# Moving four bn_stats instructions on VectorE behind the transposed exponentials, in a cross-attention and mixture-of-adapters kernel

## Chip, cores and metric

The kernel runs on one core of one Trainium2 chip. The metric is the device time of one execution in microseconds, the median of several executions.

## What is computed

There are 8 batches of 224 query rows and 750 context rows, all of width 2048, in fp32. The first part is a cross-attention whose keys are also its values; the second is a linear layer with a low-rank expert term.

```python
# x: (8, 224, 2048)   ctx: (8, 750, 2048)
n = layernorm(x)                              # mean and variance over the 2048 columns
a = einsum('bqd,bkd->bqk', n, ctx)
c = einsum('bqk,bkd->bqd', softmax(a), ctx)
x = x + c
m = layernorm(x)
base = einsum('bsi,oi->bso', m, base_w) + base_b
hidden = einsum('bsi,ri->bsr', m, A)          # r = 64
probs = softmax(einsum('bsi,ei->bse', m, router_w))   # e = 16, the two best are kept
delta = einsum('bse,bsr,eor->bso', combine(top2(probs)), hidden, B)
out = x + base + 0.5 * delta
```

## The kernel before

Every fp32 product is made of three fp32r products: each operand is split into a high part, which ScalarE (ACT) makes by copying, and a low part, which VectorE (DVE) makes by subtracting the high part from the original. TensorE (PE) then multiplies high by high, high by low and low by high.

The attention runs over the batches, one call of `one(b, stage)` in each engine's own program. Batch 0 is the stage "first", batches 1 to 6 are the stage "mid" (a loop), batch 7 is "last". The queue of transfers is on SyncE (SP). An engine works through its list strictly in the written order and meets the others only through semaphores.

A mid batch goes like this on PE. `scores_of` multiplies the normalised queries with the context (L715 to L717). Then come the transposes of the second layer norm's rows of the batch before (L752), nine of the 16 steps of the product with A and the router (`hidden_of`, L768 to L770), the transposes of the exponentials (`exps_T`, L795), and the other seven steps of `hidden_of`. In `outputs_of` PE waits until both low parts of the transposed exponentials are there (`eT_l`, L1162), and then goes through 24 value blocks e = 0 to 23, six blocks of 128 context rows for each of four chunks of 512 columns. A block takes six matmuls (L818 to L820, three for each half of the rows). Behind block 1 come two small transposes, and ahead of blocks 13, 14, 16 and 17 the transposes of the next batch's queries. In the stage "first" there is no old batch, and so no `hidden_of` and no second layer norm between the scores and the value blocks.

Block e needs the low part of its values, `raw_l`, which DVE makes in `value_low(e)` (L1176) from `val_h`, made by ACT in `value_high(e)` (L979). `val_h` has four buffers, so ACT can begin with block e when PE has finished block e - 4. Blocks 0 to 3 are prepared while the scores run.

The next batch's first layer norm is made in between. `stats` (L1180) is one bn_stats over 512 columns of `xn`; there are eight (two halves of the rows, four chunks). Then DVE aggregates them and adds epsilon at e = 6 (`ve`, L1188), GpSimd (POOL) takes the reciprocal root (`rs`, L1570), DVE makes the shift `nb` at e = 8 (L1193), and ACT waits for it in its list between `value_high(9)` and `value_high(10)`, where it normalises the first half of `xn` (L970, 2 us); the second half follows behind `value_high(10)`.

`residual(b, c)` (L1206 and L1212) is on DVE behind `value_low(6 * (c + 1) + 3)`: it takes the finished chunk out of PSUM and adds it to `x2`, which holds the batch's input rows. Its transfer is started on SP at L523.

Of the kernel before, what the change touches and what calls it, by code (L numbers as in the profile page):

```python
# [36 lines left out]
def as_f32(ap):  # L37

    return ap.bitcast(F32)
# [24 lines left out]
def xattn_ffn_kernel(nc, x, ctx, bias, ctxT, arT, wT, bT, out):  # L64
# [129 lines left out]
    with ExitStack() as stack:  # L194
        def sb(name, shape, dt=F32, of=stack):
            return of.enter_context(nc.sbuf_tensor(name, shape, dt))
# [13 lines left out]
        def sem(name):  # L210
            return stack.enter_context(nc.semaphore(name))
# [5 lines left out]
        st1 = sb("st1", [QT, NQ, CH, STATS])  # L217
# [26 lines left out]
        with ExitStack() as first:  # L244
            xn = sb("xn", [QT, NQ, D], F32, first)
# [108 lines left out]
        xn_loaded = sem("xn_loaded")  # L354
# [17 lines left out]
        stat1, aggr1, var1, rstd1, bias1 = (sem(f"ln1_{n}") for n in ("stats", "aggr", "var", "rstd", "bias"))  # L372
# [784 lines left out]
        def _(dve):  # L1157
            def low(stage, b, name, n, high_part, low_part, cols, width):

                dve.wait_ge(high_done, act_no(stage, b, name, n) + 1)  # L1160
                src = place(stage, name, n).rearrange("p (k c) -> p k c", k=cols)[:, :, 0:width]
                dve.tensor_tensor(low_part, src, as_f32(high_part), ALU.subtract).then_inc(drained, 1)  # L1162

            def ctx_low(b, j):
                dve.wait_ge(ctx_high_done, b * NPC + j + 1)
                dve.tensor_tensor(ctxT_l[:, j % LR, :, :], ctxT_in[:, j % LR, :, :],  # L1166
                                  as_f32(ctxT_h[j % HR][:, :, :]), ALU.subtract).then_inc(ctx_ready, 1)

            def four_blocks(tile, n):
                return tile[:, 4 * n:4 * n + 4, :].rearrange("p (k i) c -> p k (i c)", k=2)  # L1170

            def value_low(b, e):
                c, t = e // NT, e % NT
                dve.wait_ge(val_high, b * (CH * NT) + e + 1)
                rows = rows_of(t)
                dve.tensor_tensor(raw[0:rows, c, t, :], raw_in[0:rows, c, t, :], as_f32(val_h[0:rows, e % NR, :]), ALU.subtract).then_inc(val_ready, 1)  # L1176

            def stats(tile, st, sem_stat, i):
                q, c = i // CH, i % CH
                dve.bn_stats(st[:, q, c, :], tile[:, q, c * BANK:(c + 1) * BANK]).then_inc(sem_stat, 1)  # L1180

            def aggregate(st, mv, sem_aggr):
                for q in range(NQ):
                    dve.bn_aggr(mv[:, q, :], st[:, q, :, :].rearrange("p c s -> p (c s)")).then_inc(sem_aggr, 1)

            def variance(mv, ve, sem_aggr, sem_var, n):
                dve.wait_ge(sem_aggr, n * NQ + NQ)
                dve.tensor_scalar(ve[:, :], mv[:, :, 1], EPS, None, ALU.add).then_inc(sem_var, 1)  # L1188

            def shift(mv, rs, nb, sem_rstd, sem_bias, n):  # L1190

                dve.wait_ge(sem_rstd, n + 1)
                dve.scalar_tensor_tensor(nb[:, :], mv[:, :, 0], -1.0, rs[:, :], ALU.mult,  # L1193
                                         ALU.mult).then_inc(sem_bias, 1)

            def row_max(b):
                for q in range(NQ):
                    dve.wait_ge(scores_done, b * NQ + q + 1)
                    dve.reduce_max(nmax[:, q:q + 1], all_scores(q), AX.X,
                                   negate=True).then_inc(max_ready, 1)  # L1200
# [15 lines left out]
            def hidden_out(stage, b):  # L1216
                dve.wait_ge(filled, job_no(stage, b, "hid") + 1)
                dve.tensor_copy(hT[:, :], hid_place(stage)).then_inc(drained, 1)
# [112 lines left out]
            def one(b, stage):  # L1331
                old, new = stage != "first", stage != "last"
                x2T_low = lambda n: low(stage, b, "x2T", n, four_blocks(nT_h, n), four_blocks(nT_l, n), 2, 2 * LQ)
                for j in range(NPC):
                    if j >= HR:
                        ctx_low(b, j)
                    if stage == "first" and j in (2, 3):
                        low("pre", 0, "qT", j, four_blocks(nT_h, j), four_blocks(nT_l, j), 2, 2 * LQ)

                    if old and j < 2:  # L1340
                        if j == 0:
                            dve.wait_ge(x2_done, b * (NQ * CH))
                        for i in range(4 * j, 4 * j + 4):
                            stats(x2, st2, stat2, i)
                        if j == 1:
                            dve.wait_ge(stat2, b * (NQ * CH))
                    if old and j == 2:
                        aggregate(st2, mv2, aggr2)
                        variance(mv2, ve2, aggr2, var2, b - 1)
                    if old and j == 3:  # L1350
                        shift(mv2, rs2, nb2, rstd2, bias2, b - 1)
                    if stage == "first" and j == 3:
                        dve.wait_ge(ar_high, 1)
                        dve.tensor_tensor(ar_l[:, :, :], ar_in[:, :, :], as_f32(ar_h[:, :, :]),
                                          ALU.subtract).then_inc(ar_ready, 1)

                    if old and j >= NPC - 2:
                        x2T_low(j - (NPC - 2))
                    if j >= NPC - 2:
                        value_low(b, 2 * (j - (NPC - 2)))  # L1360
                        value_low(b, 2 * (j - (NPC - 2)) + 1)
                if old:
                    x2T_low(2)
                row_max(b)
                if old:
                    x2T_low(NX - 1)
                if new:
                    dve.wait_ge(xn_loaded, b * 16 + 16)
                    for i in range(4):
                        stats(xn, st1, stat1, i)  # L1370
                for q in range(NQ):
                    three = lambda tile: tile[:, q, :, :].rearrange("p (k i) c -> p k (i c)", k=2)
                    low(stage, b, "eT", q, three(eT_h), three(eT_l), 2, 3 * QT)
                if old:
                    hidden_out(stage, b)
                for e in range(NR, CH * NT):
                    value_low(b, e)
                    c, t = e // NT, e % NT
                    if new and e in (4, 5):
                        for i in range(2 * e - 4, 2 * e - 2):  # L1380
                            stats(xn, st1, stat1, i)
                        if e == 5:
                            dve.wait_ge(stat1, b * (NQ * CH) + 2 * NQ * CH)
                    if new and e == 6:
                        aggregate(st1, mv1, aggr1)
                        variance(mv1, ve1, aggr1, var1, b + 1)
                    if new and e == 8:
                        shift(mv1, rs1, nb1, rstd1, bias1, b + 1)
                    if old and e == HN_AT + 3:
                        hidden_back(stage, b)  # L1390
                    if not new and e in FIRST_W_AT:
                        weight_low(FIRST_W_AT.index(e))
                    if not new and e in FIRST_A_AT:
                        tile_low(0, (FIRST_A_AT.index(e),))
                    if new and e - 3 in QT_AT:
                        n = QT_AT.index(e - 3)
                        low(stage, b, "qT", n, four_blocks(nT_h, n), four_blocks(nT_l, n), 2, 2 * LQ)
                    if c >= 1 and t == 3:
                        residual(b, c - 1)
                    if not new and c >= 1 and t in (4, 5):  # L1400
                        if t == 4:
                            dve.wait_ge(x2_done, b * (NQ * CH) + c * NQ)
                        stats(x2, st2, stat2, (t - 4) * CH + c - 1)
                if new:
                    for j in range(HR):
                        ctx_low(b + 1, j)
                residual(b, CH - 1)

            def weight_low(n):
                dve.wait_ge(w_high, n + 1)  # L1410
                loaded, high_part, low_part = w_pair(n)
                dve.tensor_tensor(low_part, loaded, as_f32(high_part), ALU.subtract).then_inc(w_ready, 1)  # L1412
# [98 lines left out]
            for g in range(GT):  # L1511
                c, i = chunk_of(g), step_of(g)
# [221 lines left out]
```

## Time and profile before

| | |
|---|---|
| median of three runs | 1424.84 us (1423.66 to 1428.0) |
| time of the profiled execution | 1423.66 us |
| its span, first to last instruction | 1421.8 us |
| PE busy | 1354.5 us, 95% of the span |
| DVE busy | 935.6 us, 66% |
| ACT busy | 623.4 us, 44% |
| mean granted clock of PE | 0.993 |
| attention, first batch to the last value block | from 0 to about 670 us |
| one mid batch | about 81 us |

A row of a timeline has the start in microseconds, the duration, the engine, the line, the operation with its output and inputs, the count of merged instructions and, in brackets, how long the engine had been idle before and what it waited for. Successive instructions overlap in the records: the next may start a little before the one in front of it ends. The time of the execution is 1.86 us longer than its span. The granted clock is 1.00 when PE runs at 2.4 GHz and 0.50 at 1.2 GHz.

### The profile page before, as it was taken

The page shows a single profiled execution, that of the slowest core. Times are in us where ns is not written, and L with a number is a line of the kernel's source. Part 1 is how long each engine was busy: PE and PEld are TensorE (multiplying, and loading weights), DVE is VectorE, ACT ScalarE, POOL GpSimd, SP SyncE. Part 2 cuts the span into 40 slices and gives each one's busy share as a digit, 9 for nine tenths or more (in the row PEclk, how much of TensorE's full clock was granted, in tenths as well). Part 3 has the DMA queues.
Part 4 walks back from the last instruction along what each step waited for, and adds up shares of the span by engine and source line. Part 5 has one row for each costly group of instructions (what it writes and reads, how often), then busy time and mean ns, then how long its engine had stood idle before and what let it go on. Part 6 is the DMA issues. An engine that isn't in the chain of part 4 may idle for free.

```text
span 1421.8 us, 18364 instructions
## 1 busy us (share of the span) xinstructions
PE 1354.5 (95%) x6777; PEld 1104.8 (78%) x6777; DVE 935.6 (66%) x1179; ACT 623.4 (44%) x777; POOL 316.9 (22%) x247
## 2 busy tenths in 40 slices
PE   5899999999999999999999999988889999999998
PEld 4678888787878888786888877777677888888886
DVE  5576768788777768768465566766667745644543
ACT  3355554545564554546321366766666400100110
POOL 2002002020201102020615724434443011111110
PEclk9899999999999999999999999999999999999999
DMA  8957678687867768679658697999995988788783
GB/s 289 296 198 255 213 251 254 211 253 255 272 222 247 250 219 250 229 247 212 208 149 205 195 300 225 301 312 298 280 286 126 329 257 255 239 255 254 229 264 125
DMA packets 206520, 345.34 MB, mean 243 GB/s; under 512 B 26912, under 2 KB 119072, under 8 KB 196768
## 3 DMA queue, kind: packets, MB, share of 16 engines
q1 hardware_dynamic: 187872, 277.06, 64.3%
q0 software_dynamic: 10528, 52.85, 12.1%
q10 hardware_dynamic: 8064, 14.68, 3.0%
q8 instruction: 35, 0.57, 0.2%
q14 instruction: 21, 0.17, 0.0%
HBM read 260.87 MB, written 99.41 MB: 253 GB/s over the span
## 4 chain that ended last, share of the span: by engine, by line
PE 37%; DMA 12%; DVE 3%; issue 1%; ACT 1%; POOL 0%; SPq 0%; POOLq 0%; ACTq 0%; DVEq 0%
PE scores L849 11%; PE scores L851 11%; PE scores L850 11%; DMA res<-x_scratch 6%; DMA y_scratch<-y_out,yrow_i 4%; PE work L885 1%; PE work L886 1%; DMA w_in<-in_wT_dram 1%; DMA a_in<-xT_scratch 1%; DVE raw_l L1176 1%; ACT y_out L1077 1%; DVE w_l L1412 0%; DVE a_l L1421 0%; DVE x L1212 0%; ACT b_hl L1069 0%
## 5 line engine op out<-in xcount | busy, mean ns | idle before, releaser
L849 PE MATMUL scores<-w_h,a_h 128*128 128x512 f32 x896 | 351.9, 393 | 3.0 <-issue 3.0
L851 PE MATMUL scores<-w_h,a_l 128*128 128x512 f32 x896 | 350.9, 392 | 0.0
L850 PE MATMUL scores<-w_l,a_h 128*128 128x512 f32 x896 | 350.5, 391 | 0.0
L1053 ACT ACTIVATE a_h<-a_in 128x512 fp32r<-128x512 f32 x148 | 83.6, 622 | 319.4 <-DMA a_in<-xT_scratch 226.0
L849 PEld LDWEIGHTS scores<-w_h,a_h 128*128 128x128 f32 x896 | 168.5, 188 | 40.3 <-issue 3.4
L851 PEld LDWEIGHTS scores<-w_h,a_l 128*128 128x128 f32 x896 | 168.4, 188 | 37.5
L850 PEld LDWEIGHTS scores<-w_l,a_h 128*128 128x128 f32 x896 | 168.5, 188 | 37.0
L1421 DVE TENSOR_TENSOR a_l<-a_in,a_h 128x512 fp32r<-128x512 f32 x148 | 113.6, 814 | 122.6 <-ACT a_h L1053 119.2
L1176 DVE TENSOR_TENSOR raw_l<-raw_in,val_h 128x512 fp32r<-128x512 f32 x192 | 155.7, 828 | 49.6 <-ACT val_h L979 48.7
L715 PE MATMUL scores<-ctxT_h,nT_h 128*112 128x494 f32 (+1 forms) x512 | 174.9, 342 | 6.9 <-DVE x L1212 3.3
L717 PE MATMUL scores<-ctxT_h,nT_l 128*112 128x494 f32 (+1 forms) x512 | 171.7, 335 | 0.0
L716 PE MATMUL scores<-ctxT_l,nT_h 128*112 128x494 f32 (+1 forms) x512 | 171.5, 335 | 0.0
L979 ACT ACTIVATE val_h<-raw_in 128x512 fp32r<-128x512 f32 x192 | 119.0, 626 | 107.6 <-PE scores L820 107.6
L1166 DVE TENSOR_TENSOR ctxT_l<-ctxT_in,ctxT_h 128x1500 fp32r<-128x1500 f32 x64 | 109.5, 1719 | 85.9 <-ACT ctxT_h L957 85.2
L1593 POOL TENSOR_TENSOR res<-res,bias_b 128x512 f32<-128x512 f32 x56 | 82.0, 1465 | 372.5 <-DMA res<-x_scratch 361.5
L818 PE MATMUL scores<-val_h,eT_h 128*112 128x512 f32 (+1 forms) x384 | 156.2, 407 | 8.1 <-DVE eT_l L1162 5.8
L820 PE MATMUL scores<-val_h,eT_l 128*112 128x512 f32 (+1 forms) x384 | 152.4, 397 | 0.0
L819 PE MATMUL scores<-raw_l,eT_h 128*112 128x512 f32 (+1 forms) x384 | 152.1, 396 | 0.0
L957 ACT ACTIVATE ctxT_h<-ctxT_in 128x1500 fp32r<-128x1500 f32 x64 | 92.2, 1451 | 118.6 <-PE scores L717 108.3
L1464 DVE TENSOR_TENSOR b_hl<-b_in,b_hl 64x2048 fp32r<-64x2048 f32 x43 | 101.0, 2351 | 63.3 <-ACT b_hl L1069 62.5
L1586 POOL TENSOR_TENSOR xT_st<-nT_h,nT_l 128x896 f32<-128x896 f32 x32 | 72.5, 2272 | 167.8 <-DVE nT_l L1162 167.8
L1570 POOL TENSOR_TENSOR rs<-ve,mhalf 112x2 f32<-112x2 f32 x16 | 15.0, 936 | 425.1 <-DVE ve L1188 425.1
(149 smaller groups left out, 1971.5 us busy)
## 6 DMA issues: line engine op xcount, KB each, us to landing
ctxT_in<-in_ctxT_dram SPq DMA_DIRECT2D x64, 750.0 KB, 7.2
raw_in<-in_ctx_dram SPq DMA_DIRECT2D x32, 1280.0 KB
a_in<-xT_scratch SPq DMA_DIRECT2D x37, 1024.0 KB, 9.0
w_in<-in_wT_dram SPq DMA_DIRECT2D x32, 512.0 KB, 9.6
x<-in_x_dram SPq DMA_DIRECT2D x8, 1792.0 KB, 9.6
xT_scratch<-xT_st SPq DMA_DIRECT2D x8, 1792.0 KB, 11.9
res<-x_scratch SPq DMA_DIRECT2D x56, 256.0 KB, 7.5
y_add<-y_scratch SPq DMA_DIRECT2D x56, 256.0 KB, 5.5
```

The costliest lines, as they stand in the source:

```text
L715: pe.matmul(out, qh, ch, start=(k == 0), stop=False)
L716: pe.matmul(out, qh, cl, start=False, stop=False)
L717: last = pe.matmul(out, ql, ch, start=False, stop=(k == KD - 1))
L818: pe.matmul(out, eh, vh, start=(t == 0), stop=False)
L819: pe.matmul(out, eh, vl, start=False, stop=False)
L820: last = pe.matmul(out, el, vh, start=False, stop=(t == NT - 1))
L849: pe.matmul(o, ah, wh, start=(k == 0), stop=False)
L850: pe.matmul(o, ah, wl, start=False, stop=False)
L851: last = pe.matmul(o, al, wh, start=False, stop=(k == KD - 1))
L979: act.activation(val_h[0:rows, e % NR, :], raw_in[0:rows, c, t, :], ACT.Copy).then_inc(val_high, 1)
L1176: dve.tensor_tensor(raw[0:rows, c, t, :], raw_in[0:rows, c, t, :], as_f32(val_h[0:rows, e % NR, :]), ALU.subtract).then_inc(val_ready, 1)
L1421: dve.tensor_tensor(a_l[at][:, cols, :], a_in[at][:, cols, :], as_f32(a_h[at][:, cols, :]), ALU.subtract).then_inc(a_ready, 1)
```

## The change

Four of the eight `stats` of the next batch's `xn`, with the wait for the transfer of `xn` ahead of them, are moved on DVE from their place ahead of the low parts of the transposed exponentials to the place behind `value_low(4)` and `value_low(5)`. Four stood there altogether before, two behind each; after the change eight do, four behind each. This holds for the stages "first" and "mid". Nothing else is changed.

```diff
@@ -1364,10 +1364,6 @@
                 row_max(b)
                 if old:
                     x2T_low(NX - 1)
-                if new:
-                    dve.wait_ge(xn_loaded, b * 16 + 16)
-                    for i in range(4):
-                        stats(xn, st1, stat1, i)
                 for q in range(NQ):
                     three = lambda tile: tile[:, q, :, :].rearrange("p (k i) c -> p k (i c)", k=2)
                     low(stage, b, "eT", q, three(eT_h), three(eT_l), 2, 3 * QT)
@@ -1377,7 +1373,9 @@
                     value_low(b, e)
                     c, t = e // NT, e % NT
                     if new and e in (4, 5):
-                        for i in range(2 * e - 4, 2 * e - 2):
+                        if e == 4:
+                            dve.wait_ge(xn_loaded, b * 16 + 16)
+                        for i in range(4 * (e - 4), 4 * (e - 4) + 4):
                             stats(xn, st1, stat1, i)
                         if e == 5:
                             dve.wait_ge(stat1, b * (NQ * CH) + 2 * NQ * CH)
```

## Rows read from the trace of the kernel before

**Rows 1.** Who waited for whom, PE, 150 to 640 us: total, times, longest.

```profile
PE scores L768 <- ACT prob L984: 3.4, 6, 0.6
PE scores L715 <- DVE x L1212: 2.8, 6, 0.5
PE scores L715 <- DVE ctxT_l L1166: 2.2, 6, 0.4
```

**Rows 2.** Timeline, PE, batch 2: the first matmul of value blocks 0, 6 and 11.

```profile
228.34 0.45 PE L818 MATMUL scores<-val_h,eT_h 128*112 128x512 f32 x1
...
236.88 0.40 PE L818 MATMUL scores<-val_h,eT_h 128*112 128x512 f32 x1
...
243.87 0.40 PE L818 MATMUL scores<-val_h,eT_h 110*112 110x512 f32 x1
```

**Rows 3.** Timeline, ACT, batch 2.

```profile
225.79 1.35 ACT L951 ACTIVATE eT_h<-work 128x672 fp32r<-128x672 f32 x2 [2.02 <-PE work L795]
...
237.62 2.09 ACT L970 ACTIVATE xn<-xn,nb,rs 112x2048 f32<-112x2048 f32 x1
...
242.12 1.66 ACT L979 ACTIVATE val_h<-raw_in 110x512 fp32r<-110x512 f32 x3
```

**Rows 4.** Timeline, DVE, batch 2.

```profile
223.94 2.46 DVE L1180 BATCH_NORM_STATS2 st<-xn 112x6 f32<-112x512 f32 x4
226.56 1.62 DVE L1162 TENSOR_TENSOR eT_l<-work,eT_h 128x672 fp32r<-128x672 f32 x2
...
231.25 1.28 DVE L1180 BATCH_NORM_STATS2 st<-xn 112x6 f32<-112x512 f32 x2
232.45 0.68 DVE L1176 TENSOR_TENSOR raw_l<-raw_in,val_h 110x512 fp32r<-110x512 f32 x1
...
234.78 0.68 DVE L1176 TENSOR_TENSOR raw_l<-raw_in,val_h 128x512 fp32r<-128x512 f32 x1
...
237.18 0.16 DVE L1193 SCALAR_TENSOR_TENSOR nb<-mv,rs 112x2 f32<-112x2 f32 x1
...
242.76 2.66 DVE L1176 TENSOR_TENSOR raw_l<-raw_in,val_h 110x512 fp32r<-110x512 f32 x4 [1.81 <-ACT val_h L979]
```

**Rows 5.** Timeline, POOL, batch 2.

```profile
236.04 1.10 POOL L1570 TENSOR_TENSOR rs<-ve,mhalf 112x2 f32<-112x2 f32 x1 [9.83 <-DVE ve L1188]
```

**Rows 6.** Timeline, PE, batch 0: last transposes, value blocks 0 and 10.

```profile
56.86 0.79 PE L795 MATMUL work<-ident,prob 112*128 112x112 f32 x6 [1.27 <-ACT prob L984]
63.48 0.77 PE L818 MATMUL scores<-val_h,eT_h 128*112 128x512 f32 x1 [5.83 <-DVE eT_l L1162]
...
80.34 0.39 PE L818 MATMUL scores<-val_h,eT_h 128*112 128x512 f32 x1
```

**Rows 7.** Timeline, ACT, batch 0.

```profile
57.69 0.73 ACT L951 ACTIVATE eT_h<-work 128x672 fp32r<-128x672 f32 x1 [0.26 <-PE work L795]
```

**Rows 8.** Timeline, DVE, batch 0.

```profile
59.43 2.48 DVE L1180 BATCH_NORM_STATS2 st<-xn 112x6 f32<-112x512 f32 x4 [3.63 <-DMA xn<-in_x_dram]
61.82 1.61 DVE L1162 TENSOR_TENSOR eT_l<-work,eT_h 128x672 fp32r<-128x672 f32 x2
...
76.48 1.41 DVE L1212 SCALAR_TENSOR_TENSOR x<-scores,rinv,x 112x512 f32<-112x512 f32 x2
```

**Rows 9.** The line L523 on SP, 50 to 60 us: issue, and time to landing.

```profile
L523 SPq DMA_DIRECT2D x<-in_x_dram x1: 432/432/432, 51.1 to 51.1; - x1
...
DMA to landing us min/median/max: 23.2/23.2/23.2
```

**Rows 10.** Windows: length, busy PE, PEld, DVE, ACT, POOL (instructions); then granted clock, DMA share, GB/s.

```profile
58.00:60.00 2.00, 0.00 (x0) 0.00 (x0) 0.57 (x1) 0.42 (x1) 0.00 (x0) 0.85 0.96 339
68.00:70.00 2.00, 2.00 (x7) 1.47 (x6) 1.33 (x3) 0.63 (x1) 0.00 (x0) 0.59 0.99 221
970.00:974.00 4.00, 4.00 (x13) 3.05 (x12) 1.74 (x1) 2.23 (x2) 3.51 (x4) 0.59 1.00 342
1010.00:1014.00 4.00, 4.00 (x19) 3.31 (x19) 2.16 (x1) 1.81 (x1) 2.56 (x3) 1.00 1.02 357
```

## The prediction

> **What bounds the kernel now.** I read the list of waits on PE first. Over six batches, 150 to 640 us, PE waits three times in each batch, for 3.4 + 2.8 + 2.2 = 8.4 us altogether, and none of these waits is for the moved instructions [rows 1]. All three are links of a chain that starts from PE's own work, so they give nothing back when PE comes late. PE therefore sets the time of the attention: a delay of PE there is a delay of the end, and a gain is a gain, unless a transfer that PE does not drive comes between.
>
> Then I read the timelines of the three engines around the start of the value blocks, for batch 2. Batches 1 and 6 have the same distances to within 0.02 us, so batch 2 stands for all six mid batches. Batch 0 I read by itself, because it has no product with A to cover the exponentials.
>
> **The change in a mid batch: what it removes.** The four stats run from 223.94 to 226.40, and the low parts of the exponentials begin at 226.56 [rows 4]. They could hardly begin earlier: the two high parts run on ACT from 225.79 to 227.14 together, so the first ends near 226.5 [rows 3]. The second low part ends at 228.18, and PE begins with block 0 at 228.34 with no idle time, out of its own earlier products [rows 2, 4]. DVE gains an idle stretch there, and PE gains nothing. I cost the removal at zero.
>
> **What it adds in a mid batch.** Between `value_low(4)` and `value_low(6)` there are four more stats. Two of them hold up the next instruction by 232.45 - 231.25 = 1.20 us [rows 4], so one costs 0.60 us of DVE's list and four cost 2.40 us. The Trainium skill (VectorE: DVE Perf Modes, The DRAIN you can't avoid) says that the next operation does not start until the pipeline has emptied. Taken literally, each stats would cost its full duration, about 0.68 us, the shift would be 2.7 us and the batch would lose 2.1 us instead of the 1.8 worked out below; the trace differs, since the next instruction starts before the recorded end. The sum goes by 0.60.
>
> The wait for `xn` moves too, and `value_low(5)` and all later ones are queued behind it. It holds nothing up: the same data were there at 223.94, and the new place is reached at 231.25 [rows 4].
>
> `value_low(5)` starts 1.20 us later, ends at 232.45 + 1.20 + 0.68 = 234.33, and block 5 starts on PE one block (1.40 us, from (243.87 - 236.88) / 5, [rows 2]) ahead of 236.88, at 235.48. That is covered with 1.1 us to spare.
>
> *First stall, block 6.* `value_low(6)` started at 234.78 and now starts at 237.18; it ends at 237.86 [rows 4]. PE starts some 0.05 us behind the end of what it waits for (63.43 to 63.48, [rows 6, 8]), so at 237.91. Without a wait it started at 236.88 [rows 2]. Stall: 1.03 us.
>
> *Second stall, block 11.* Everything behind block 6 on DVE is later by 2.40 us as long as it hangs on the stats: the variance, POOL's root of 1.10 us behind it [rows 5], and `nb`, which ended at 237.34 [rows 4] and now ends at 239.74. ACT started to normalise `xn` at 237.62 [rows 3] because it was busy until then; now it waits for `nb` until 239.78, which is 2.16 us later. Two normalisations of 2 us each and `value_high(10)` stand in its list ahead of `value_high(11)`, back to back from 237.62 to 242.12 [rows 3]. So `value_low(11)` moves from 242.76 to 244.92, ends near 245.60 [rows 4], and block 11 starts at 245.65. PE would be there at 243.87 + 1.03 = 244.90. Stall: 0.75 us. Before, the same instruction ended at 243.44 and was covered by 0.43 us.
>
> Block 7 is ready at about 238.98 and wanted at 239.31; block 10 is ready at 243.1 and wanted at 243.5. Both are close, neither costs. Behind block 12 ACT and DVE need about 0.6 us for a block of 1.40 us and have caught up before the transposes ahead of block 13. SP's store of the small hidden rows waits for `hn`, which is 2.4 us later; behind it stand reloads of values that wait for block 12 anyway.
>
> Per mid batch 1.03 + 0.75 = 1.78 us, and six of them 10.7 us. The bounds: the second stall could be absent if ACT's normalisation is not really held (1.03 each, 6.2 us), and with 0.68 us for each stats it is 2.1 each, 12.5 us.
>
> **Batch 0: the gain.** Here DVE waits for the transfer of `xn` until 59.43, does the four stats, and only then the low parts; PE is idle for 5.83 us [rows 6, 8]. Without them the second low part follows the second high part, which ends at 58.42 [rows 7]; it takes 0.8 to 0.9 us (two take 1.61), so PE starts at 59.36 instead of 63.48, 4.12 us earlier. The clock may add to that. It fell to half within 58 to 60 us (0.85 over that window) and came back only at 69.6 (0.59 over 68 to 70) [rows 10], so that 6.1 us of PE's work ran at half speed and cost 3.1 us. Whether it falls again when PE starts at 59.36 I can't tell from the rows.
>
> It does not matter, because something else is late next. `residual(0, 0)`, at block 9, needs the batch's input rows in `x2`. Their transfer is issued at 51.1 and lands 23.2 us later, at 74.3 [rows 9]; before, DVE came to it at 76.48 [rows 8] and did not wait. Now DVE comes there at 71 to 73, waits until 74.3, and `value_low(10)` is queued behind: two residual steps to 75.7, the low part to 76.35, block 10 at 76.4. PE would want block 10 between 59.36 + 14.0 + 0.7 = 74.1 (full clock, one stall at block 6) and 59.36 + 16.86 = 76.2 (the pace of before, 80.34 - 63.48, [rows 6]). In both cases the transfer decides. Block 10 started at 80.34, so the gain is 3.9 us. Bounds: 4.1 + 3.1 - 1.8 = 5.4 us if the transfer landed earlier, and nothing if reloads that now start earlier share the engines with it and delay it by 3.9 us. Behind block 10 nothing is ahead of the stream of transfers, and the gain lasts.
>
> **Sum.** 10.7 - 3.9 = 6.8 us on the profiled execution's 1423.66 us: 1430.5 us. The median of the runs shown, 1424.84, is 1.2 us above that execution, so against it the change is +5.7 us or 0.4%. Differences under about 0.3%, 4.3 us, can hardly be told from none here.
>
> **Rivals.**
> *A, the forecast:* two stalls in each mid batch, gain of about 3.9 in batch 0; 1430.5 us, own range 1427.5 to 1433.5. Chance 0.62.
> *B, only block 6 stalls.* ACT would have to come to block 11 in time. For it speaks that the cover was 0.43 us and the first stall adds 1.03 more; against it that 2.16 us of shift exceed both. 6.2 - 3.9 = +2.3, 1426.0 us. Chance 0.14.
> *C, the opposite side: DVE has room for the stats at block 6, and only batch 0 counts.* The place is `value_low(6)`, the price per mid batch s, and it decides at 6 s = 3.9, s = 0.65 us. If s is zero the time is 1419.8 us. For it: DVE idles 1.7 us ahead of `value_low(4)`. Against it: that idle time lies ahead of the stats, where ACT waits for PE, and can't be used; behind it `value_low(6)` ended 236.88 - 235.46 = 1.42 us ahead of its use, and 2.40 us are put in [rows 2, 4]. Chance 0.08.
> *D, the clock falls in each mid batch.* After a pause of 3.2 us ahead of 970 us the clock stood at 0.59 over the next 4 us; after one of 2.3 us ahead of 1010 us it stayed at 1.00 [rows 10]. The new pauses are 1.03 and 0.75 us with 7 us of matmuls between, which speaks against it. At 3.1 us for each fall it would be 18.6 us more, 1449 us. The Trainium skill (TensorE: Matmul & The Clock Gate, HAM oscillation) describes this pattern, a pause in every tile that throttles every tile again. Chance 0.07.
> *E, batch 0 gains nothing,* because the transfer into `x2` is pushed back; +10.7, 1434.4 us. Chance 0.09.
>
> **The numbers.** The likeliest case gives 1430.5. The range from 1425.0 to 1436.0 holds A, B and E and leaves C and D out, and takes in 12.5 us for the stalls with no more than 1 us of gain. Slower by over 0.3%: A but for its lower end (0.57), D and E, 0.73. Within 0.3%: the rest of A, B and half of C, 0.23. Faster: 0.04.
>
> **What the profile after would show.** PE waits for `raw_l` 12 times in the six mid batches, about 1.0 us at block 6 and 0.75 at block 11; `nb` 2.4 us later against block 0; the wait for `eT_l` in batch 0 near 1.7 us instead of 5.83; DVE waiting there for the transfer into `x2` at about 74.3, and PE for `raw_l` at block 10. What would make it wrong: another pace of the stats than 0.60 us, an ACT that gets `nb` earlier than I think, or a landing of `x2` that moves with the earlier reloads.

## The result and the profile after

The changed kernel took 1437.26 us (median of 14 runs, 1430.12 to 1441.65); the kernel before took 1428.41 us (14 runs, 1422.90 to 1433.29) beside it. The ratio is 1.0063, with a 95% interval from 1.0045 to 1.0081: the change makes the kernel slower, by 8.85 us between the medians. I had forecast slower by 5.7 us against the median then known. The time lies 1.3 us above the range.

The profiled execution after took 1436.82 us, with a span of 1433.4 us. The whole attention part ends later by 9.2 us: the first matmul of the expert part starts at 680.02 us instead of 670.83. What follows took 753.4 us instead of 750.9. (In other traces of these kernels the same part took 750.9 to 759.0 us, so that single number says nothing. Between the two profiled executions lie 13.2 us: 9.2 in the attention, 2.4 in the expert part, and 1.5 outside the span.)

PE's waits over the six mid batches, the view of [rows 1]:

```profile
PE scores L818 <- DVE raw_l L1176: 8.4, 12, 0.9
PE scores L768 <- ACT prob L984: 3.5, 6, 0.6
PE scores L715 <- DVE x L1212: 2.8, 6, 0.5
PE scores L715 <- DVE ctxT_l L1166: 2.2, 6, 0.4
```

Three lines are as they were, to within 0.1 us. One is new: twelve waits for `raw_l`, two in each mid batch. The timelines of batch 2 show where. PE, against [rows 2]:

```profile
228.22 0.45 PE L818 MATMUL scores<-val_h,eT_h 128*112 128x512 f32 x1
...
236.07 0.39 PE L818 MATMUL scores<-val_h,eT_h 110*112 110x512 f32 x1
237.77 0.49 PE L818 MATMUL scores<-val_h,eT_h 128*112 128x512 f32 x1 [0.85 <-DVE raw_l L1176]
238.56 0.39 PE L818 MATMUL scores<-val_h,eT_h 128*112 128x512 f32 x1
...
244.12 0.39 PE L818 MATMUL scores<-val_h,eT_h 128*112 128x512 f32 x1
245.53 0.49 PE L818 MATMUL scores<-val_h,eT_h 110*112 110x512 f32 x1 [0.55 <-DVE raw_l L1176]
246.31 0.39 PE L818 MATMUL scores<-val_h,eT_h 110*112 110x512 f32 x1
```

DVE and ACT in the same batch, against [rows 3, 4]:

```profile
226.43 1.62 DVE L1162 TENSOR_TENSOR eT_l<-work,eT_h 128x672 fp32r<-128x672 f32 x2 [2.53 <-ACT eT_h L951]
...
231.14 2.47 DVE L1180 BATCH_NORM_STATS2 st<-xn 112x6 f32<-112x512 f32 x4
233.52 0.68 DVE L1176 TENSOR_TENSOR raw_l<-raw_in,val_h 110x512 fp32r<-110x512 f32 x1
234.11 2.47 DVE L1180 BATCH_NORM_STATS2 st<-xn 112x6 f32<-112x512 f32 x4
...
237.04 0.68 DVE L1176 TENSOR_TENSOR raw_l<-raw_in,val_h 128x512 fp32r<-128x512 f32 x1
...
239.43 0.16 DVE L1193 SCALAR_TENSOR_TENSOR nb<-mv,rs 112x2 f32<-112x2 f32 x1
...
244.79 2.50 DVE L1176 TENSOR_TENSOR raw_l<-raw_in,val_h 110x512 fp32r<-110x512 f32 x4 [1.81 <-ACT val_h L979]
```

```profile
239.63 2.10 ACT L970 ACTIVATE xn<-xn,nb,rs 112x2048 f32<-112x2048 f32 x1 [2.03 <-DVE nb L1193]
241.63 0.61 ACT L979 ACTIVATE val_h<-raw_in 128x512 fp32r<-128x512 f32 x1
242.15 2.08 ACT L970 ACTIVATE xn<-xn,nb,rs 112x2048 f32<-112x2048 f32 x1
244.14 2.17 ACT L979 ACTIVATE val_h<-raw_in 110x512 fp32r<-110x512 f32 x4
```

This trace of batch 2 lies 0.12 us ahead of the old one (block 0 at 228.22 against 228.34). With that taken out, `raw_l` of block 6 starts 237.04 - 234.78 + 0.12 = 2.38 us later, `nb` 2.37 us later, the normalisation 2.13 us later, and `raw_l` of block 11 2.15 us later. The low parts of the exponentials, freed of the stats, start no earlier: DVE now idles 2.53 us for ACT there.

The distance between the first exponentials of two successive mid batches gives the loss as a whole. Before, from 140.05 to 221.12 us:

```profile
140.05 0.89 ACT L984 ACTIVATE prob<-scores,nmax 112x750 f32<-112x750 f32 x1 [3.46 <-DVE nmax L1199]
...
221.12 0.89 ACT L984 ACTIVATE prob<-scores,nmax 112x750 f32<-112x750 f32 x1 [3.48 <-DVE nmax L1199]
```

After:

```profile
138.06 0.89 ACT L984 ACTIVATE prob<-scores,nmax 112x750 f32<-112x750 f32 x1 [3.50 <-DVE nmax L1199]
...
220.99 0.89 ACT L984 ACTIVATE prob<-scores,nmax 112x750 f32<-112x750 f32 x1 [3.48 <-DVE nmax L1199]
```

That is 81.07 and 82.93 us; over the six mid batches the distances are 81.03 to 81.07 before and 82.89 to 82.95 after. One mid batch loses 1.88 us, six lose 11.3 us.

In batch 0 PE after the change, against [rows 6]:

```profile
57.10 0.79 PE L795 MATMUL work<-ident,prob 112*128 112x112 f32 x6 [1.27 <-ACT prob L984]
59.61 0.67 PE L818 MATMUL scores<-val_h,eT_h 128*112 128x512 f32 x1 [1.71 <-DVE eT_l L1162]
...
69.94 0.49 PE L818 MATMUL scores<-val_h,eT_h 128*112 128x512 f32 x1 [0.19 <-DVE raw_l L1176]
...
78.26 0.48 PE L818 MATMUL scores<-val_h,eT_h 128*112 128x512 f32 x1 [2.47 <-DVE raw_l L1176]
```

And DVE, against [rows 8]:

```profile
76.20 1.41 DVE L1212 SCALAR_TENSOR_TENSOR x<-scores,rinv,x 112x512 f32<-112x512 f32 x2 [3.19 <-DMA x<-in_x_dram]
```

The wait for the exponentials is 1.71 us instead of 5.83. The clock still fell, but came back sooner: the window from 60 to 62 us stood at 0.50, 62 to 64 at 0.71, 64 to 66 at 1.00. Then DVE waited 3.19 us for the transfer into `x2`, and PE 2.47 us for DVE at block 10. From the first exponentials of batch 0 to those of batch 1 it took 84.05 us instead of 86.29, a gain of 2.24 us.

### The profile page after: what moved, and what is told of

Read it like the earlier page. It is cut to its first block, busy times and chain, and to the rows that moved or that the text cites. A ratio compares the mean times of both kernels' runs of the same rounds, so it can differ in the third digit from the quotient of the medians.

```text
span 1433.4 us, 18364 instructions
## 1 busy us (share of the span) xinstructions
PE 1361.7 (95%) x6777; PEld 1106.7 (77%) x6777; DVE 935.2 (65%) x1179; ACT 623.8 (44%) x777; POOL 320.4 (22%) x247
## 4 chain that ended last, share of the span: by engine, by line
PE 35%; DMA 11%; DVE 3%; issue 2%; ACT 2%; POOL 1%; SPq 0%; ACTq 0%; POOLq 0%; DVEq 0%
PE scores L849 11%; PE scores L850 11%; PE scores L851 11%; DMA res<-x_scratch 5%; DMA y_scratch<-y_out,yrow_i 5%; PE work L885 1%; DMA w_in<-in_wT_dram 1%; PE work L886 1%; ACT b_hl L1069 1%; ACT y_out L1077 1%; DVE a_l L1419 1%; DVE raw_l L1176 1%; DMA hs_scratch<-hg,pos_i 0%; DVE w_l L1410 0%; DVE b_hl L1462 0%
## 5 line engine op out<-in xcount | busy, mean ns | idle before, releaser
L1419 DVE TENSOR_TENSOR a_l<-a_in,a_h 128x512 fp32r<-128x512 f32 x148 | 110.5, 794 | 103.8 <-ACT a_h L1053 100.2
```

The lines of the kernel that those rows point to most:

```text
L1419: dve.tensor_tensor(a_l[at][:, cols, :], a_in[at][:, cols, :], as_f32(a_h[at][:, cols, :]), ALU.subtract).then_inc(a_ready, 1)
```

## The experiments

Diffs are against the kernel after the change unless said otherwise; `...` marks lines left out. Landing means the time from the issue of a transfer until its data are there. Experiments 3 to 7 are one execution each and are read by their traces alone.

**1 and 2: the change by stages.** The first kernel moves the stats in batch 0 alone, the second in batches 1 to 6 alone.

```diff
 # batch 0 alone (in the other kernel "mid" and "first" change places)
+                if stage == "mid":
+                    dve.wait_ge(xn_loaded, b * 16 + 16)
+                    for i in range(4):
+                        stats(xn, st1, stat1, i)
...
                     if new and e in (4, 5):
-                        if e == 4:
+                        moved = not (stage == "mid")
+                        if e == 4 and moved:
                             dve.wait_ge(xn_loaded, b * 16 + 16)
-                        for i in range(4 * (e - 4), 4 * (e - 4) + 4):
+                        for i in (range(4 * (e - 4), 4 * (e - 4) + 4) if moved else range(2 * e - 4, 2 * e - 2)):
                             stats(xn, st1, stat1, i)
```

> The four bn_stats are moved in batch 0 alone; batches 1 to 6 stay as before. My theory (two stalls in each mid batch cost 11.3 us, batch 0 gains 2.2 us): the distance between the first exponentials of two mid batches is 81.03 us as before, the one from batch 0 to batch 1 about 84.0 us (86.29 before), the execution about 2 us or 0.15% faster than before. Rival (the loss comes from the low parts of batch 0 or from the expert part behind the attention): the distances are the same, but the execution is slower than before by some 9 us.

Measured: ratio 0.9987 to the kernel before, interval 0.9973 to 1.0002, median 1427.90 against 1430.53 us. The mid distances are 81.03 to 81.06 us. But from batch 0 to batch 1 it took 86.34 us in the trace, not 84.0: the transfer into `x2` landed 25.6 us behind its issue, PE stood still for 3.15 us at block 10, and then the clock fell, though the pause was only 0.7 us longer than after the change. The first matmul of block 10, and two windows with the columns of [rows 10]:

```profile
79.02 0.49 PE L818 MATMUL scores<-val_h,eT_h 128*112 128x512 f32 x1 [3.15 <-DVE raw_l L1176]
...
80.00:82.00 2.00, 2.00 (x6) 1.46 (x5) 1.02 (x3) 0.63 (x1) 0.00 (x0) 0.53 0.13 40
82.00:84.00 2.00, 2.00 (x7) 1.40 (x7) 0.44 (x1) 0.35 (x1) 0.00 (x0) 0.62 0.02 9
```

> The four bn_stats are moved in batches 1 to 6 alone; batch 0 stays as before. My theory: mid distance 82.9 us, batch 0 to batch 1 86.3 us, PE waits 12 times for raw_l in the mid batches, the execution 11.3 us or 0.8% slower than before. Rival (the mid stalls are given back behind the attention): under 5 us slower.

Measured: ratio 1.0080, interval 1.0054 to 1.0106, median 1440.64 us. Mid distances 82.90 to 82.96 us, and the waits are there without the change in batch 0:

```profile
PE scores L818 <- DVE raw_l L1176: 8.3, 12, 0.9
```

The whole loss, 11.4 us by the ratio (7.7 to 15.2 by its interval) and 11.3 us by the trace, is in the mid batches, and nothing behind the attention gives it back. The two ratios add up to 0.67%, against 0.63% for the whole change. The gain in batch 0 is small and unsteady; experiments 5 to 9 look for why.

**3: the second normalisation later.** This separates the two stalls.

```diff
-LN1_AT = (9, 10)
+LN1_AT = (9, 12)
```

> As after the change, but ACT does the second normalisation of xn behind value_high(12) instead of value_high(10). My theory (block 11 waits because two normalisations that start 2.2 us late stand ahead of value_high(11)): only block 6 stalls, by about 1.0 us plus 0.09 us of restart; mid distance 82.1 us instead of 82.91. Rival (block 11 is late because DVE itself is behind): the stall at block 11 stays and the distance is 82.9 us.

Measured: distances of 82.13 to 82.16 us, and six waits instead of twelve.

```profile
PE scores L818 <- DVE raw_l L1176: 5.1, 6, 0.9
```

ACT, batch 2: three value blocks (10, 11, 12) now pass between the two normalisations.

```profile
237.48 2.10 ACT L970 ACTIVATE xn<-xn,nb,rs 112x2048 f32<-112x2048 f32 x1 [2.04 <-DVE nb L1193]
239.49 1.66 ACT L979 ACTIVATE val_h<-raw_in 128x512 fp32r<-128x512 f32 x3
241.05 2.09 ACT L970 ACTIVATE xn<-xn,nb,rs 112x2048 f32<-112x2048 f32 x1
```

The stall at block 11 is gone and the one at block 6 is untouched (0.85 us of idle time). DVE is not what is late at block 11; ACT's order is. The first stall alone costs 82.14 - 81.04 = 1.10 us, the second 82.92 - 82.14 = 0.78 us.

**4: half the dose.** Two of the four stats stay early, and three follow each of the value blocks 4 and 5.

```diff
+                if new:
+                    dve.wait_ge(xn_loaded, b * 16 + 16)
+                    for i in range(2):
+                        stats(xn, st1, stat1, i)
...
-                        if e == 4:
-                            dve.wait_ge(xn_loaded, b * 16 + 16)
-                        for i in range(4 * (e - 4), 4 * (e - 4) + 4):
+                        for i in range(3 * e - 10, 3 * e - 7):
                             stats(xn, st1, stat1, i)
```

> Two bn_stats ahead of the low parts of the exponentials, three behind value_low(4), three behind value_low(5): half the dose. My theory: value_low(6) is 1.2 us later than before and has 1.42 us of cover, so block 6 doesn't stall; nb is 1.2 us later, ACT's normalisation about 0.96 us, and block 11 stalls by about 0.58 us plus 0.09; mid distance 81.7 us. Rival (the cost grows evenly with the number of bn_stats moved): half of 1.88 us, distance 81.97 us with a stall at block 6. Batch 0 as before the change, since it waits for xn again, and about 86 us to batch 1.

Measured: distances of 81.71 to 81.78 us, one wait in each batch, and it is at block 11:

```profile
246.06 0.48 PE L818 MATMUL scores<-val_h,eT_h 110*112 110x512 f32 x1 [0.45 <-DVE raw_l L1176]
```

Half the stats cost 0.7 us and the whole 1.88: the cost is what exceeds a cover, not a share for each instruction. Batch 0, where DVE waits for `xn` ahead of the exponentials again, was no repeat of the old trace: the transfer into `x2` landed 25.6 us behind its issue, and even here DVE had to wait for it (0.79 us). So a late landing needs no early start of the value blocks.

**5: the change once more.**

> The changed kernel once more, for the spread of a single trace. My theory: the six mid distances are 82.9 us again and the stalls 0.85 and 0.55 us of idle; the landing of the transfer into x2 in batch 0 comes 24 to 26 us behind its issue, as after the change (24.8) and in the run with the change in batch 0 alone. Rival (the late landing was chance): it comes 23 us behind, as before the change.

Measured: mid distances of 82.91 to 82.95 us. The transfer landed 25.5 us behind its issue, and this time batch 0 lost: 87.32 us to batch 1. This time the clock did not fall at block 0 (0.49 us for its first matmul, against 0.67), so PE came to block 10 earlier and met a later landing there. It stood still for 4.24 us, and now the clock fell.

```profile
79.30 0.77 PE L818 MATMUL scores<-val_h,eT_h 128*112 128x512 f32 x1 [4.24 <-DVE raw_l L1176]
```

Windows of 2 us with the columns of [rows 10]:

```profile
75.00:77.00 2.00, 0.06 (x1) 0.00 (x0) 0.00 (x0) 2.00 (x3) 0.00 (x0) 1.00 1.00 357
77.00:79.00 2.00, 0.00 (x0) 0.00 (x0) 1.76 (x3) 0.81 (x2) 0.00 (x0) 0.85 0.77 288
79.00:81.00 2.00, 1.70 (x4) 1.33 (x5) 2.00 (x4) 0.00 (x0) 0.00 (x0) 0.50 0.50 137
81.00:83.00 2.00, 2.00 (x6) 1.39 (x6) 0.15 (x2) 0.63 (x1) 0.00 (x0) 0.50 0.09 34
83.00:85.00 2.00, 2.00 (x7) 1.39 (x6) 0.59 (x1) 0.20 (x1) 0.00 (x0) 0.50 0.00 1
85.00:87.00 2.00, 2.00 (x15) 1.68 (x13) 1.54 (x3) 0.97 (x2) 0.00 (x0) 0.95 0.50 76
```

From the restart at block 10 to the exponentials of batch 1 it took 141.76 - 79.30 = 62.46 us, against 138.06 - 78.26 = 59.80 us in the first trace after the change, where the pause was 2.47 us and the clock stayed. The longer pause cost 2.7 us beyond itself. The pause of 3.15 us in experiment 1 cost 1.55 us beyond itself (140.37 - 79.02 = 61.35), while pauses of 0.68 us in experiment 3 and 1.73 us in experiment 6 cost nothing (59.84 and 59.81). The gate that the change opened in batch 0 leads straight into a second one, and a longer wait there can take the gain back.

**6: is the landing late because a reload starts earlier?** The first reload of values waits for the transfer into `x2`.

```diff
                     load_ctxT(b + 1, LR - 1)
+                    if first:
+                        sp.wait_ge(xres_loaded, 16)
                     raw_again(b, 0)
```

> As after the change, but in batch 0 SP starts the first reload of values only when the transfer into x2 has landed. My theory (the reload, started 5 us earlier than before the change, shares the engines with the last part of the transfer into x2 and delays it): it lands 23.2 us behind its issue, as before the change, block 10 starts 1.5 us earlier, and batch 0 to batch 1 takes 82.5 us instead of 84.05. Rival (the landing varies by chance, or with what was queued before): 24.8 us and 84.05 us as without the hold.

Measured: landing 24.0 us behind the issue, 83.22 us to batch 1. Between the two expectations, and it does not stand alone: the kernel of experiment 3, which has no hold, had a landing of 23.1 us, the kernels of experiments 2 and 4, where the reload starts as late as before the change, 24.1 and 25.6. My theory of the reload is not borne out: four traces with the early reload have a mean landing of 24.75 us (23.1 to 25.6), four with a late or held one 24.2 us (23.2 to 25.6). Single traces with such a spread can't exclude a share of some tenths of a microsecond. The landing varies from trace to trace between 23.1 and 25.6 us, while the 16 DMA engines are all busy from about 36 us until it comes; what sets it within that range stays open.

**7: the transfer into `x2` ahead of the next context blocks.**

```diff
                     sp.dma_start(xn[:, :, :], x_v[b + 1]).then_inc(xn_loaded, 16)
+                    if first:
+                        sp.dma_start(x2[:, :, :], x_v[b]).then_inc(xres_loaded, 16)
...
                 if not first:
                     sp.wait_ge(filled, job_no(stage, b, "x2T", NX - 1) + 1)
-                sp.dma_start(x2[:, :, :], x_v[b]).then_inc(xres_loaded, 16)
+                    sp.dma_start(x2[:, :, :], x_v[b]).then_inc(xres_loaded, 16)
```

> As after the change, but in batch 0 the transfer into x2 is issued right behind the one of xn, ahead of three blocks of the next batch's context. My theory (this transfer decides block 10): it lands before 72 us, the wait for it is gone, block 10 starts near 75.7 us; block 11 then waits for the two normalisations, until about 78.3 us, so that batch 0 to batch 1 takes 82.5 us instead of 84.05. Rival (DVE or ACT decide block 10): 84 us.

Measured: issued at 40.9, landed at 68.1 us; no wait for it. Batch 0 to batch 1 took 82.41 us, and the one wait left at the value blocks behind block 0 is at block 11, behind the two normalisations:

```profile
78.44 0.48 PE L820 MATMUL scores<-val_h,eT_h 110*112 110x512 f32 x1 [0.86 <-DVE raw_l L1178]
```

The transfer did decide block 10. At block 11 the two normalisations stand ahead, as in a mid batch; experiment 8 moves the second one.

**8: a version that beats both.** The stats are moved in batch 0 alone (experiment 1), with its transfer earlier (experiment 7) and its second normalisation behind block 12. The diff shows the last part, which is new.

```diff
+                    ln1_at = (9, 12) if stage == "first" else LN1_AT
-                    if stage != "last" and e in LN1_AT:
-                        if e == LN1_AT[0]:
+                    if stage != "last" and e in ln1_at:
+                        if e == ln1_at[0]:
```

> The change in batch 0 alone, with its transfer into x2 issued right behind the one of xn, and its second normalisation behind value_high(12). My theory: mid distance 81.03 us, batch 0 to batch 1 81.1 us (86.29 before: 4.1 us of earlier start, 1.4 us less at half clock, 0.3 us of stall at block 6), the execution 5 us or 0.36% faster than before the change. Rival (what batch 0 gains is lost to later transfers): 1% of nothing, within 0.1% of before, with a longer distance from batch 0 to batch 1 or later ones.

Measured: ratio 0.9953 to the kernel before, interval 0.9934 to 0.9971, median 1423.37 against 1430.00 us. Batch 0 to batch 1 took 80.38 us, 5.9 us less than before; mid distances 81.04 to 81.08 us. PE's waits at the value blocks of batch 0 are down to the exponentials and 0.56 us at block 6:

```profile
60.23 0.48 PE L820 MATMUL scores<-val_h,eT_h 128*112 128x512 f32 x1 [1.71 <-DVE eT_l L1165]
69.39 0.49 PE L820 MATMUL scores<-val_h,eT_h 128*112 128x512 f32 x1 [0.56 <-DVE raw_l L1179]
```

Block 0 took 0.48 us here and not 0.67 as after the change: the clock did not fall in this trace. After the change its fall made the first nine matmuls of the value blocks 1.6 us longer (63.35 - 59.61 against 62.39 - 60.23 here), so this alone is enough for the 0.7 us by which the gain exceeds the expectation.

The trace shows one thing more. Of its 5.9 us only 1.2 are left at the first matmul of the expert part (669.59 us against 670.83), and this execution, 1431.72 us, was the slowest of the twelve. Of the rest 0.9 us lie ahead of the first exponentials, and 3.65 us are lost in batch 7, which none of the kernels changes: there ACT waits for the transfer into `a_in` (line of the kernel, then the total, the times and the longest wait in us). Before:

```profile
ACT a_h L1053 <- DMA a_in<-xT_scratch: 2.0, 1, 2.0
```

and here:

```profile
ACT a_h L1056 <- DMA a_in<-xT_scratch: 4.4, 1, 4.4
```

Over all eleven traces this wait goes from 1.5 to 5.3 us, and the stretch from the first exponentials of batch 7 to the expert part from 44.0 to 49.1 us, longer where the wait is longer (in one pair by 0.1 us the other way). The same kernel gave 1.9 and 3.7 us (after the change and experiment 5). So it is the twelve runs, and not this one execution, that show the gain in the kernel's time. What the later normalisation gives by itself was not run.

**9: the earlier transfer alone, in the kernel before the change** (the diff of experiment 7).

> The kernel before the change, with nothing but batch 0's transfer into x2 issued right behind the one of xn. Two readings of why the change in batch 0 alone gained only 0.13%, and with the earlier transfer and the later normalisation 0.47%. Mine: the gain was held by the landing of this transfer, and the kernel before mostly did not wait for it (it came there at 76.5 us in its trace), so that the earlier transfer alone gives the old kernel little: 0 to 0.15% faster, batch 0 to batch 1 still 85.5 to 86.5 us, the wait for the low part of the exponentials 5.8 us or a little more. Rival: the late landing alone was what cost the old kernel its time, and the earlier transfer gives most of the 0.47% by itself.

Measured: ratio 1.0019, interval 1.0005 to 1.0032, slower by about 2.7 us (2.0 between the medians) and not faster. The old order waits for `xn` first, and that transfer came later:

```profile
60.98 2.47 DVE L1182 BATCH_NORM_STATS2 st<-xn 112x6 f32<-112x512 f32 x4 [5.08 <-DMA xn<-in_x_dram]
```

In the old trace it was there at 59.43 [rows 8]. That its new neighbour in the queue delays it is likely but not shown: `xn` landed 21.0 us behind its issue here and 19.5 in the old trace, but over the seven other traces that do not move `x2` it took 19.2 to 21.0 us. PE's wait for the exponentials grew to 7.26 us, and batch 0 to batch 1 took 86.92 us. The rival falls, and so does my 0 to 0.15% of gain: the same edit goes with a shorter batch 0 where the stats are late and with a slower kernel where they are early.

| kernel | batch 0 to 1, us | mid distance, us | landing of `x2` behind its issue, us |
|---|---|---|---|
| before | 86.29 | 81.04 | 23.2 |
| after | 84.05 | 82.92 | 24.8 |
| after, again (5) | 87.32 | 82.93 | 25.5 |
| batch 0 alone (1) | 86.34 | 81.04 | 25.6 |
| mid batches alone (2) | 85.56 | 82.93 | 24.1 |
| second normalisation later (3) | 82.35 | 82.14 | 23.1 |
| two stats early (4) | 85.88 | 81.75 | 25.6 |
| reload held (6) | 83.22 | 82.93 | 24.0 |
| `x2` earlier (7) | 82.41 | 82.93 | 27.2, issued 10 us earlier |
| version that beats both (8) | 80.38 | 81.07 | 26.8, issued 10 us earlier |
| old kernel, `x2` earlier (9) | 86.92 | 81.05 | 27.5, issued 10 us earlier |

## Why the prediction was right and where it was wrong

*Removal costs and gains nothing in a mid batch: right.* DVE waits 2.53 us for ACT in the freed place, and PE starts block 0 as before.

*0.60 us for each stats: right.* Four took 2.38 us of DVE's list. The Trainium skill (VectorE: DVE Perf Modes, The DRAIN you can't avoid) says that the next operation does not start until the pipeline is empty, and adds that one that is not held starts earlier. The first half alone, as my prediction quoted it, would have made it 2.7 us; the trace agrees with the second.

*The first stall, 1.03 us at block 6, and the second, 0.75 at block 11: right in place and in cause.* The starts came 1.00 and 0.71 us later than the pace allows (237.77 - 236.07 - 0.70, 245.53 - 244.12 - 0.70). Experiment 3 removed the second alone; experiment 4 removed the first and left 0.71 us of the second. Both stalls stand in the trace, which rules out B, and experiment 2 shows their cost in the kernel's time, which rules out C.

*What was missing: the restart.* After a wait the first matmul lasts 0.49 instead of 0.39 us, and the next starts 0.79 instead of 0.70 us behind it: 0.09 us for each stall, twelve times, 1.1 us in all. The six mid batches lose 11.3 and not 10.7 us.

*The step that failed: "the gain is 3.9 us" in batch 0.* I had the second gate right, block 10 behind the transfer into `x2`. But I took its landing, 23.2 us behind the issue, as a number of the kernel, when it was one draw of a spread from 23.1 to 25.6. Counted from the exponentials of batch 0 to the start of block 10, 26.58 us before, the five traces with all four stats moved and the transfer in its old place gained this:

| | landing, us | gain up to block 10, us |
|---|---|---|
| second normalisation later (3) | 23.1 | 4.07 |
| reload held (6) | 24.0 | 3.17 |
| after | 24.8 | 2.33 |
| after, again (5) | 25.5 | 1.72 |
| batch 0 alone (1) | 25.6 | 1.59 |

What the landing adds, the gain loses, and with the landing that I assumed about my 3.9 us would have come out. I had also put the clock behind block 10 at nothing, with the words "the gain lasts": pauses of 3.15 and 4.24 us there cost another 1.55 and 2.7 us. The gain over the whole batch was 2.24 us in the profiled execution and a loss of 1.0 in the next; measured over runs, batch 0 alone gives 0.13% or 1.9 us, with an interval from a gain of 3.9 to a loss of 0.3. That the new early reload pushes the transfer back (my lower bound and rival E) is not supported by experiments 2, 3, 4 and 6, nor excluded as a small share. E's outcome, no gain in batch 0, did come in two traces, by the spread and the clock.

*The sum.* 11.3 - 2.2 = 9.1 us in the trace, 8.85 us between the medians, against 6.8 forecast. Of the 2.3 us between 9.1 and 6.8, 1.7 are the landing and 0.6 the mid batches. But the time is 6.8 us above the 1430.5 that I gave, and only 2.05 of these are the change; the other 4.75 are the start of the sum, 1423.66 us, one execution that lies 4.75 us under the median of 14. The range missed by 1.3 us; it would have held the same change of 8.85 us from the 1424.84 us that was known beforehand (1433.7). The kernel before stood at 1428.41 us over 14 runs, 3.6 us above the three runs that I had; its own spread, 1422.9 to 1433.3, was wider than they showed, and the range left no room for it. Part of that spread is batch 7 and the expert part (experiment 8). That the 9.1 us of one pair of traces and the 8.85 us of the medians agree within 0.3 us is in part luck, since batch 0 alone moved by 3.3 us between two traces of the changed kernel.

*Clock.* Rival D is out: over the mid batches no window fell, with pauses of 0.85 and 0.55 us. In batch 0 it mattered, and what I had left open stays open: over the seven traces with all four stats moved there, block 0 started at 59.3 to 60.2 us, and the clock fell within its first blocks in five of them and not in two.

## What to carry to other kernels

An engine that is busy where nothing waits is not a cost; ask how much cover the place has to which its work is moved, and follow each instruction that is queued behind it, on the next engine too: 2.4 us moved into 1.42 us of cover gave one stall, and a 2 us normalisation that started late on ACT gave a second five blocks on. An opened gate is worth the distance to the next gate only, and when that one is a transfer, its landing is a range and has to be read from more than one trace. A one-time stage at the start and a loop body can want opposite orders: here moving the stats in batch 0 alone, with its transfer into `x2` earlier and its second normalisation later, gains 0.47%, and moving them in the loop loses 0.8%.

## What the runs showed of the hardware

A transfer of 1792 KB into `x2`, issued at 51.1 to 52.4 us behind the same queue of transfers in eight traces, landed 23.1 to 25.6 us later. At the value blocks of batches 0 to 6, after pauses of 0.19 to 3.15 us, the next matmul of 128x512 lasted 0.48 to 0.49 us at full clock instead of 0.39; in the mid batches the group behind it came 0.09 us late. In eleven traces ACT's wait for the first transfer into `a_in` in batch 7 took 1.5 to 5.3 us. Pauses of up to 2.47 us at block 10 left the clock at full speed; one of 3.15 us was followed by half clock about 1 us behind the restart and cost a further 1.55 us, one of 4.24 us was followed by half clock at the restart and cost 2.7 us.
